# Graph units: turns, projections, values and outputs in other rounds, and another table of places for the maxima

## The reference

```python
for c in range(NUM_NOD):
    nsrc = min(c + 1, MAX_PREV)
    ...
    q = ew[c, 0] * (nodes[in_q] @ We[eq] + be[eq])
    k = ew[c, 1] * (nodes[in_k] @ We[ek] + be[ek])
    v = ew[c, 2] * (nodes[in_v] @ We[ev] + be[ev])
    o = _mha(q, k, v, Wq[c], Wk[c], Wv[c], Wo[c])
    nodes[c] = act_w[c] * o + q
    lind += nsrc
```

## Time and profile before

| | |
|---|---|
| median of 3 runs | 3035.99 us (3026.24 to 3041.26) |
| profiled execution | 3025.15 us, of which the span is 3022.9 |
| TensorE busy in the span | 2844.8 us (94%) |
| VectorE | 2364.1 us (78%) |
| ScalarE | 2158.6 us (71%) |
| GpSimd | 383.0 us (13%) |
| mean granted TensorE clock | 0.978 |
| first graph unit starts | at 814.9 us of the span |

### The profile page before, as it was taken

One profiled execution on the slowest core, in us unless ns is written; L12 is line 12 of the kernel. 1 busy time (PEld: TensorE's weight loads), 2 busy tenths in 40 slices (PEclk: granted clock), 3 DMA queues, 4 the chain that ended last, 5 costly groups with the idle time before them and its releaser, 6 DMA issues. The chain is left out here.

```text
span 3022.9 us, 48974 instructions
## 1 busy us (share of the span) xinstructions
PE 2844.8 (94%) x18943; PEld 1285.0 (43%) x18943; DVE 2364.1 (78%) x2964; ACT 2158.6 (71%) x2739; POOL 383.0 (13%) x328
## 2 busy tenths in 40 slices
PE   6899999998699999999999999999999999999993
PEld 4556666654333333333333333333333333333321
DVE  7656556666788888888888888888888888888833
ACT  3556556555377888887888788878787878887782
POOL 0000000000011111111111111111011111011014
PEclk8999999999799999999999999999999999999996
DMA  7000000013424444345344445354445444444202
GB/s 172 13 9 16 15 12 12 5 62 72 93 63 111 101 97 94 96 92 116 97 105 89 99 88 116 98 114 78 104 87 111 104 110 76 107 100 95 52 23 92
DMA packets 146989, 241.57 MB, mean 80 GB/s; under 512 B 56834, under 2 KB 97174, under 8 KB 143430
## 3 DMA queue, kind: packets, MB, share of 16 engines
q1 hardware_dynamic: 146758, 238.46, 35.4%
HBM read 163.58 MB, written 72.03 MB: 78 GB/s over the span
## 5 line engine op out<-in xcount | busy, mean ns | idle before, releaser
L1659 ACT ACTIVATE pt_b<-ps_max 128x1024 f32<-128x1024 f32 x1516 | 1489.7, 1024 | 285.4 <-PE ps_max L1524 281.0
L1684 DVE TENSOR_REDUCE mx_b<-ps_pair 128x2 f32<-128x1024 f32 (+1 forms) x989 | 1192.2, 1205 | 105.7 <-PE ps_pair L1512 94.8
L1559 PE MATMUL ps_ctx<-pt_b,vs 128*32 128x512 f32 x6144 | 818.9, 605 | 3.8 <-ACT c_b L1648 3.5
L1684 DVE TENSOR_REDUCE mx_b<-ps_misc 128x1 f32<-128x512 f32 x989 | 677.1, 685 | 161.9 <-PE ps_misc L1512 158.2
L1524 PE MATMUL ps_max<-qs,ks 50*128 50x512 f32 x3032 | 764.9, 432 | 4.6 <-ACT pt_b L1659 1.2
L1512 PE MATMUL ps_pair<-ks,qs 48*128 48x512 f32 x1955 | 524.5, 463 | 23.7 <-DVE mx_b L1684 22.0
L1512 PE MATMUL ps_misc<-ks,qs 48*128 48x512 f32 x989 | 446.6, 452 | 12.6 <-DVE mx_b L1684 7.7
L1524 PEld LDWEIGHTS ps_max<-qs,ks 50*128 50x128 f32 x3032 | 345.4, 185 | 227.6 <-ACT pt_b L1659 140.1
L1512 PEld LDWEIGHTS ps_pair<-ks,qs 48*128 48x128 f32 x1955 | 202.2, 184 | 378.7 <-DVE mx_b L1684 352.5
L1512 PEld LDWEIGHTS ps_misc<-ks,qs 48*128 48x128 f32 x989 | 182.5, 185 | 380.9 <-DVE mx_b L1684 310.6
L930 ACT ACTIVATE pt<-ps_max,cb 128x512 f32<-128x512 f32 x340 | 214.9, 686 | 180.0 <-PE ps_max L657 117.4
(11 more groups left out here) (199 smaller groups left out, 2172.0 us busy)
## 6 DMA issues: line engine op xcount, KB each, us to landing
partd<-part SPq DMA_DIRECT2D x22, 2048.0 KB, 9.3
qs<-partd SPq DMA_DIRECT2D x288, 128.0 KB, 5.7
ks<-partd SPq DMA_DIRECT2D x288, 128.0 KB, 6.7
xv<-node SPq DMA_DIRECT2D x26, 512.0 KB, 5.5
xf<-node SPq DMA_DIRECT2D x24, 512.0 KB, 4.7
node<-nt_b SPq DMA_DIRECT2D x48, 256.0 KB, 2.1
rec_b<-invd SPq DMA_DIRECT2D x368, 32.0 KB, 1.8
xq<-node SPq DMA_DIRECT2D x22, 512.0 KB, 3.7
```

Of the source, the lines that this page charges most:

```text
L1559: ins = pe.matmul(psO[SLOT * i:SLOT * i + SLOT, :], vs[u % 2][:, kb, QUAD * (s // HALF_STEPS) + i], pt[:, (QUAD * S + i) % ENTRIES], start ...
L1659: act.activation(pt[:, e:e + 2].rearrange("p k n -> p (k n)"), at[:], ACT.Exp, scale=SCALE_B).then_inc(exp_done, 1)
L1684: nc.vector.tensor_reduce(mx2[:, at:at + n], (psP, psX)[p % 2][:, 0:CHUNK * n].rearrange("p (h n) -> p h n", h=n), AX.X, ALU.max).then_inc ...
```

## The change

The places of the ten rounds in `PLAN` and of most pieces in `PIECE_SLOT` are other ones. The turn of the running unit's second half goes from round 2 to 6, the first output from 8 to 9, the projections from 11, 14, 17, 20 to 11, 18, 23, 26, the second output from 24 to 31, values from 30 and 34 to 34 and 39, the next unit's turn from 50 to 49. The first unit's turn goes from 3 to 6. The number of rounds and pieces stays, and no instruction differs.

```diff
-        PLAN = {2: ("turn", 0, 1), 8: ("output", -1, 0), 11: ("project", 2, 0), 14: ("project", 2, 1), 17: ("project", 2, 2),
-                20: ("project", 2, 3), 24: ("output", -1, 1), 30: ("values", 1, 0), 34: ("values", 1, 1), 50: ("turn", 1, 0)}
-        FIRST_PLAN = {**PLAN, 0: ("values", 0, 0), 1: ("values", 0, 1), 3: ("turn", 0, 1)}
-        del FIRST_PLAN[2]
+        PLAN = {6: ("turn", 0, 1), 9: ("output", -1, 0), 11: ("project", 2, 0), 18: ("project", 2, 1), 23: ("project", 2, 2), 26: ("project", 2, 3),
+                31: ("output", -1, 1), 34: ("values", 1, 0), 39: ("values", 1, 1), 49: ("turn", 1, 0)}
+        FIRST_PLAN = {**PLAN, 0: ("values", 0, 0), 1: ("values", 0, 1)}
         LAST_PLAN = {**PLAN, 63: ("output", 0, 0)}
...
-        PIECE_SLOT = (2, 2, 4, 6, 9, 10, 12, 14, 16, 19, 19, 21, 24, 25, 26, 27, 29, 31, 32, 33, 35, 37,
-                      38, 40, 42, 43, 45, 46, 48, 50, 50, 53, 54, 56, 58, 59, 61, 63, 64, 67, 68, 69, 70, 72,
-                      73, 77, 77, 78, 81, 83, 84, 86, 89, 90, 92, 94, 95, 98, 99, 101, 103, 104, 105, 108, 108, 111,
-                      112, 113, 116, 117, 119, 120, 121, 124, 125, 129, 130, 132, 133, 136, 137, 140, 141, 143, 144, 146)
+        PIECE_SLOT = (1, 2, 4, 7, 8, 10, 12, 14, 17, 18, 18, 19, 19, 24, 25, 27, 29, 30, 32, 33, 34, 36,
+                      37, 39, 40, 43, 44, 45, 48, 49, 50, 51, 53, 55, 57, 58, 61, 62, 64, 64, 66, 68, 70, 71,
+                      72, 75, 76, 77, 79, 81, 84, 85, 86, 89, 90, 91, 94, 96, 98, 101, 103, 105, 107, 108, 111, 111,
+                      112, 113, 116, 119, 119, 122, 123, 124, 127, 127, 128, 129, 132, 134, 136, 137, 141, 142, 144, 147)
```

## The result

The changed kernel takes 3023.18 us (median of 16 runs, 3010.12 to 3031.19), the kernel before, run beside it, 3034.16 (16 runs, 3026.24 to 3041.26). The ratio is 0.9965, 95% interval 0.9953 to 0.9977: it is 11 us faster, in the direction that was forecast, where 26 was forecast (3010). The time lies in the range, but less than half of the gain came. 0.35% is also less than the 0.5% that the prediction took for measurable; with 16 runs of each it is told from none.

A forecast was written before the change was run, and what follows sets the result against it. TensorE was taken as the bound, by its matmul starts, with removable waits on two maxima buffers read by VectorE. 21 x 1.1 + 2.9 = 26 us off the 3035.99 median gave 3010 us, range 2996 to 3032.

The forecast's parts named there:

- The method and the price of bursts: TensorE's score and maxima matmuls between full-array steps: 0.43 us for the first pair, some 0.24 per further pair or odd one.
- The plain part of 85.0: Per middle unit on TensorE: all bursts at their price plus full-array work, 85.0 us, unchanged by the new order.
- The waits, one by one: TensorE bursts over their price, mostly awaiting a maxima buffer VectorE must read: 5.1 us per unit before, 4.0 after.
- Normalisation: GpSimd's normalisation, on which the second output waits: spare time grows from 0.4 to about 3 us; effect taken at 0.
- Denominators: SyncE's DMAs behind the later turn, feeding round 10's VectorE reciprocal: hidden with 0.35 us spare; loss 0, upper bound 2 us.
- rival B: Denominators behind the later turn reach round 10 late in each unit: 52 us lost against 26 won, 3062 us; chance 0.08.
- Rival A, density: Denser pieces in rounds 12 to 33 make VectorE the bound: 0.7 to 1.0 of 1.1 lost, 3020 to 3034; chance 0.18.
- Rival C: Waits removed at four-piece bursts reappear in the next context step, exps being the true partner: about 3034 us; chance 0.06.
- First unit, -1.2: First graph unit, whose early bursts hold four to six pieces: about 1.2 us less by the same prices.
- Unit 22, -1.7: Unit 22, which spreads pieces evenly: 1.7 us less, from two bursts and 0.8 us of price fewer, some waits added.
- The last unit: The last unit, which has no pieces: change of 0, within 1 us.

The follow-up runs named there:

- e1: Changed kernel with GpSimd's third normalisation of a unit waiting until VectorE's combine of the last maxima is done: 3014.78 us, ratio 0.9916 to the kernel before.
- e4: Kernel before with GpSimd's third normalisation released when all context steps of the unit but the last are done: 3044.92 us, ratio 1.0021 to the kernel before.
- e3: Changed kernel with the denominators' DMAs issued ahead of the second half's maxima rows on SyncE: 3017.76 us, ratio 0.9934 to the kernel before.
- e13: Changed kernel with both the GpSimd wait and the denominators ahead of the maxima rows: 3012.66 us, ratio 0.9911 to the kernel before; repeated, 3010.97 us, 0.9904.
- before again: The kernel before, unedited, run and profiled once more: ratio 0.9987, middle units 1894.7 us, first unit 105.4 us.
- h1: Kernel before up to round 43, then the changed piece places and the turn in round 49: ratio 1.0017 to the kernel before.

## Why the prediction was right in direction and too large in size

Rows of before are named where they carried the step.

- **The method and the price of bursts: right.** Undisturbed units are 89.0 to 89.1, and with both disturbances removed all but one are. The plain part of 85.0 plus waits of 4.0 came out as such.
- **The waits, one by one: right, with small misses.** p17 to p19, p63 to p65 and p73 to p75 took 0.57 over the price each, p68 to p70 0.88; the four-piece burst is gone; the sum of all waits is 3.95 where 4.0 stood. Not foreseen was a wait of 0.20 in the burst of p42, s54 and p43, made good by the small ones.
- **Normalisation "had 0.4 us to spare before; now about 3. All taken at 0": this step failed.** I asked only who waits for GpSimd's result (the second output) and not what its instructions do to the engine beside them. Rounds 68 to 73 now take 6.4 us instead of 7.0, since the three pieces of p81 to p83 are gone from them, and the piece ahead of the inverses' reciprocal has two blocks in place of one (some 0.5). Both bring the normalisation nearer to the unit's end, 1.0 to 1.1 us together (the reciprocal that it depends on starts 5.8 us ahead of the end of every middle unit before, 4.7 after), and it lands on the combine. The term was put at 0; it is 12 meetings at 0.58, 7 of the missing 12 us. e1 took them away (-6.3), e4 put them into the kernel before (+9.5 to +11.0).
- **Denominators: the chain was right, its spread was looked for in the wrong place, and the value taken was wrong.** Forecast for a unit: SyncE from 8.16, last issue 12.5, landed 14.2, reciprocal 14.57; measured in unit 8: 8.11, 12.50, 14.23, 14.63. I had bounded the lateness by 2 us from one long issue of maxima rows in five and then took 0. The waits are 2.4 us in four units (4, 7, 20 and 22), but no issue of maxima rows was long: in three of the four the last DMA landed after 2.8 to 3.2 us and not 1.73 (the earlier trace rows has up to 3.5), and in unit 22 SyncE began 0.9 later. That the bound came near is luck. Without these waits the middle units are 1.2 to 2.4 us shorter (e3, and e1 against e13). With 0.35 us to spare and a known spread, some loss had to stand in the sum. That is what is left of rival B, which needed 1.5 us in every unit to turn the sign.
  By the 2.0 us for a DMA that the Trainium skill states ("DMA: Bandwidth & Descriptors", Anatomy of one DMA) they would have landed at 14.5; the trace has 1.73 and decides.
- **Rival A, density: not seen.** Bursts of five in rounds 12 to 33 closed after 0.89 to 0.95, with no wait beyond those of the sum. (Its range was also added up wrongly: 0.7 to 1.0 in 21 units, on top of 3010, is 3025 to 3031, not 3020 to 3034.) **Rival C: not seen**; the four-piece wait of the earlier trace rows is gone and did not come back.
- **First unit, -1.2: it came out at +1.3.** Its length follows the clock as well as the order. Unit 0 from its start to its end, columns as in the earlier trace rows, the clock third from the end. Kernel before:

```profile
814.86:913.90 99.04, 92.78 (x546) 38.68 (x546) 81.91 (x98) 72.91 (x88) 9.46 (x9) 0.92 0.29 71
```

Kernel after:

```profile
824.46:924.85 100.39, 94.60 (x546) 38.45 (x547) 82.17 (x98) 72.98 (x88) 8.57 (x8) 0.91 0.27 67
```

e4, which has the order of before:

```profile
821.42:921.43 100.01, 93.75 (x547) 38.62 (x547) 81.81 (x98) 72.87 (x88) 8.57 (x8) 0.91 0.28 70
```

The granted share ranges from 0.94 (e1, 98.5 us) to 0.86 (before again, 105.4 us) and lower, so two profiles of different clocks say nothing of a term of 1.2 us: of the +1.3 about 1.0 is the clock (an estimate: some 16 us of the unit at 1.2 GHz before, 18 after, each worth half). At the same 0.91 the order of after takes 100.4 (100.4 in e3 too) and that of before 100.0 (100.2 in h1). The gain that I counted is not there.
- **Unit 22, -1.7: measured -0.15.** A mis-sized term. I counted waits and left out that a score which stands behind a waiting piece adds its own 0.24 after the wait: [p11 s16 p12 p13 s18] is 0.80 over its price and not 0.57, and the last piece of p7 to p10 adds the same.
- **The last unit** moved by -0.5, within the bound of 1.

The account of the graph part: -26 forecast, +7 meetings, +2 denominators, +2.5 first unit, +1.5 unit 22, -0.5 last unit gives -13.5, and 13.7 was measured. Of these the meetings are shown by adding them and by taking them away, the denominators by taking them away. The rest is read from profiles only, and the first unit's part is in good part its clock.

## What to carry to other kernels

When a step moves on one engine, ask also what it will lie beside on its neighbour: place every GpSimd instruction of a microsecond or so against the short two-input VectorE instructions on the critical chain, and give it a fixed order behind them (here 0.3 to 0.4 us later, at no cost) rather than leave a race to chance. A unit that comes in two lengths, and in other units when run again, is the sign of such a race, and the minimum of the duration in the line of the instruction against its longest shows where. If a step has less to spare than the known spread of what it waits for, take the loss in the sum and not only in the range.

## What the runs showed of the hardware

- A VectorE TENSOR_TENSOR of 128x32 with both inputs in SBUF, 0.217 us, takes 1.25 to 1.35 if a GpSimd TENSOR_TENSOR of 1.28 has started 0.12 us ahead or less, and less with a longer lead (0.67 at 0.69, 0.29 at 1.06); it ends 0.07 to 0.08 after it. The other way round GpSimd, 0.04 behind, pays 0.03. Where the two start 0.01 apart either can come first: in e3 once VectorE's took 1.35, once GpSimd's. TENSOR_REDUCE from PSUM beside GpSimd's next instruction keeps its 1.21.
- Of such a delay only what exceeds some 0.45 us reaches the critical chain. Delays of 0.25 and 0.45 in the kernel before (units 13 and 4) and of 0.50 in its second profile cost nothing, 0.61 cost some 0.15, 0.84 and 0.87 cost 0.35 to 0.45 (second profile, units 13, 19 and 3), 1.05 costs 0.58. Of the 0.45, 0.35 is what VectorE would have idled before the next maximum (in the undisturbed unit 8).
- The start of the graph part varies by 14 us with the same instructions ahead of it. Three profiles start early (before 814.9, e1 810.6, h1 815.2), the other nine between 821.4 and 824.5. In the window of 40 to 80 us the early ones have a granted clock of 0.71 or 0.72; the late ones have 0.50 or 0.51, that is 1.2 GHz for nearly all of it. What decides which a run gets stays open. A pair of profiled spans can therefore differ by 10 us for no reason in the diff, as this one did.
